# The second attention in sixteen overlapped units, with its half sums added by GpSimd

## What is computed

```python
for Wa, ba in ((W_att0, b_att0), (W_att1, b_att1)):
    kv = bitnet_linear(image_embeds, Wa, ba)          # 361 x 128 for each batch
    k = jnp.concatenate([kv, kv], axis=-1)            # 256 wide, both halves the same
    scores = jnp.einsum('bse,bpe->bsp', fused, k) * inv_sqrt_e
    attn = jax.nn.softmax(scores, axis=-1)
    fused = fused + 0.1 * jnp.einsum('bsp,bpe->bse', attn, k)
```

## Time and profile before

| | us |
|---|---|
| median of 3 runs | 997.46 (996.68 to 1001.53) |
| profiled execution, its own time | 992.82 |
| profiled execution, span from first to last instruction | 991.0 |
| attention, from its first PE instruction to the reduction L1487 | 745.62 to 855.73 |

### The profile page before, as it was taken

The page is one execution under the profiler, slowest core; times in us unless marked ns, Lnnn a source line. Parts: engine busy times, 40 slices in busy tenths (PEclk is TensorE's granted clock), DMA queues, the critical chain, the costliest instruction groups (busy, mean ns, idle before and its releaser), DMA issues.

```text
span 991.0 us, 22346 instructions
## 1 busy us (share of the span) xinstructions
PE 821.7 (83%) x8198; PEld 604.3 (61%) x8198; DVE 725.7 (73%) x1496; ACT 556.1 (56%) x1147; POOL 292.6 (30%) x238
## 2 busy tenths in 40 slices
PE   3777888988898777798899999986647888769995
PEld 2345666666666554587666777772125777549994
DVE  7568787787877898767566776636995666776865
ACT  3446666666665436433555556538975555573542
POOL 3336444353441515040421110007603000053400
PEclk9978999999999777999999999995557888889998
DMA  6423443334453346323275555534200000200002
GB/s 182 106 67 75 97 105 91 100 105 111 121 115 81 82 167 225 110 57 115 74 200 163 163 166 167 142 102 120 71 10 0 2 0 0 85 0 2 3 1 67
DMA packets 76991, 90.47 MB, mean 91 GB/s; under 512 B 22166, under 2 KB 64945, under 8 KB 76842
## 3 DMA queue, kind: packets, MB, share of 16 engines
q1 hardware_dynamic: 69562, 80.95, 29.6%
q0 software_dynamic: 6144, 7.42, 2.8%
q10 hardware_dynamic: 1216, 1.18, 0.4%
HBM read 73.86 MB, written 15.43 MB: 90 GB/s over the span
## 4 chain that ended last, share of the span: by engine, by line
PE 54%; DVE 24%; issue 8%; ACT 7%; DMA 3%; POOL 2%; SPq 1%; ACTq 0%; DVEq 0%; POOLq 0%
PE ps L1151 11%; PE ps L1138 8%; PE ps L337 4%; PE ps L527 4%; PE ps L425 3%; PE ps L1655 3%; PE ps L499 3%; DVE p L515 3%; PE ps L569 3%; DVE m L485 2%; PE ps L2099 2%; PE ps L480 2%; PE ps L1649 2%; PE ps L2110 1%; DVE pmax L1616 1%
## 5 line engine op out<-in xcount | busy, mean ns | idle before, releaser
L485 DVE TENSOR_REDUCE m<-ps 100x2 f32<-100x722 f32 x128 | 115.2, 903 | 52.9 <-PE ps L480 51.3
L506 ACT ACTIVATE p<-ps 128x800 f32<-128x800 f32 x128 | 106.8, 835 | 43.0 <-PE ps L499 40.0
L1200 ACT ACTIVATE hT<-ps,cols 128x500 f32<-128x500 f32 (+1 forms) x96 | 62.5, 651 | 106.4 <-PE ps L1138 98.3
L1151 PE MATMUL ps<-w_h,hT_h 128*125 128x256 f16 (+1 forms) x384 | 105.9, 276 | 7.4 <-DVE x L1247 6.8
L515 DVE SCALAR_TENSOR_TENSOR p<-p 128x600 f32<-128x600 f32 x128 | 107.0, 838 | 0.0
L1207 DVE TENSOR_TENSOR hT_l<-hT,hT_h 128x500 f16<-128x500 f32 (+1 forms) x96 | 62.3, 652 | 60.9 <-ACT hT_h L1201 60.9
L1151 PE MATMUL ps<-w_h,hT_l 128*125 128x256 f16 (+1 forms) x384 | 105.9, 276 | 0.0
L1151 PE MATMUL ps<-w_l,hT_h 128*125 128x256 f16 (+1 forms) x384 | 105.8, 276 | 0.0
L1043 POOL DMA_INDIRECT xe<-tokens,slot_of x32 | 43.1, 1347 | 155.4 <-PE ps L1161 102.1
L1138 PE MATMUL ps<-xe_h,w_h 128*128 128x500 f16 (+1 forms) x192 | 71.7, 374 | 14.3 <-ACT hT_h L1201 6.1
L499 PE MATMUL ps<-qs,ks 128*128 128x100 f16 x768 | 64.7, 215 | 14.3 <-ACT p L506 14.3
(11 more groups left out here) (342 smaller groups left out, 2209.4 us busy)
## 6 DMA issues: line engine op xcount, KB each, us to landing
sw<-in_L_ffn_w_dram SPq DMA_DIRECT2D x16, 512.0 KB, 6.3
sw<-in_L_ffn_w_dram SPq DMA_DIRECT2D x8, 1024.0 KB, 5.9
k_parts<-kp SPq DMA_DIRECT2D x32, 192.0 KB, 2.0
ks<-k_parts SPq DMA_DIRECT2D x32, 192.0 KB
stage<-in_L_xattn_W_f_dram SPq DMA_DIRECT2D x6, 1024.0 KB, 7.4
ctx_f<-in_ctxT_dram SPq DMA_DIRECT2D x16, 270.8 KB, 3.1
stage<-in_ctxT_dram SPq DMA_DIRECT2D x8, 541.5 KB, 8.6
area<-in_ctxT_dram SPq DMA_DIRECT2D x16, 270.8 KB, 6.2
```

Of the source, the lines that this page charges most:

```text
L485: v.tensor_reduce(m32[p][:, 2 * i:2 * i + 2], ps[0:T, at:at + 2, 0:KV], AX.X, ALU.max).then_inc(m_max, 1)
L506: s.activation(p32[:, i % HALF, :, :, :].rearrange("p j n t -> p n j t"), ps[:, t_bank(i):t_bank(i) + 2, 0:(KJ + 1) * T].rearrange("p n (j ...
L1151: i = pe.matmul(bank[4 + j % 3][0:m, 0:C], hTp[p][hh][:, f, j * m:(j + 1) * m], w2p[of][ww][:, f, :], start=(f == 0 and hh == ww), stop=(f ...
L1200: s.activation(hT[:, f % 3, 0:m], bank[2 + f % 2][:, 0:m], ACT.Silu, bias=bias, scale=1.0 / WS)
```

## The change

The attention is written out (no loop) as sixteen units `u` of two batches and one round. `unit_of(u)` gives the pair of batches and the round: units 0 and 1 are pairs 0 and 1 with `r` = 0, units 2 and 3 the same pairs with `r` = 1, and so on. On PE the list of a unit is: scores of `u`; product of values and probabilities of `u` - 1 (both batches into one of banks 6 and 7); values, then keys, of `u` + 1; transposes of `u`. ACT's list is: exponentials of `u`, keys of `u` + 1, copies of `u`. DVE's is: scores of `u`, normalise the first batch, update `fused` for `u` - 1 (one instruction for both batches), normalise the second batch, values of `u` + 1. The tiles of a unit are two of the four (`at_slot`). `f12` is made by POOL, one 128 x 200 addition for a unit, in two buffers. The four additions of `x_b2_gpsimd` stand behind `f12` of units 3, 5, 7 and 9. The roundings of batches 8, 10, 12 and 14 on ACT and 5 to 15 on DVE stand inside the attention, behind given units (`ROUND_ACT`, `ROUND_DVE`). The maximum over `fused` is split: the last group of four batches is taken in two halves, and that of the image averages is taken ahead of the attention. The diff, where the bodies that the listing above shows are cut:

```diff
@@ -1451,9 +1451,13 @@
         neg_s = [over_vis(T, KV) for _ in range(Q)]
         prob = [over_vis(T, KP) for _ in range(Q)]
         probT = [over_vis(KT, KJ, T) for _ in range(Q)]
-        f12 = [over_vis(128, T) for _ in range(Q)]
+        f12 = [over_vis(128, 2 * T) for _ in range(2)]
         small = over_vis(T, 3, Q)
         txt_q = over_vis(128, CC * NTOK // 2).bitcast(F16).rearrange("p (c n) -> p c n", c=CC)
+
+        UNITS = B
+        ROUND_ACT = {2: 8, 4: 10, 6: 12, 8: 14}
+        ROUND_DVE = {0: 5, 1: 7, 3: 9, 4: 11, 6: 13, 8: 15}
 
         ULP = 2.0 ** -24
         CTX, VIS, IMG_, TEXT, CAT, HID = range(6)
@@ -1617,100 +1621,163 @@
                             ).then_inc(c_pm, 1)
 
 
+        def unit_of(u):
+
+            return 2 * (u // 4) + u % 2, u % 4 // 2
+
+        def pair_tokens(pair):
+            return slice(2 * pair * T, 2 * (pair + 1) * T)
+
+        def at_slot(u, q):
+            return 2 * (u % 2) + q
+
         def att_tensor(pe):
-            def body(t, *_):
...
+            def keys_values(u):
+                if u == UNITS:
+                    return
+                pair, r = unit_of(u)
+                if u % 4 == 0:
+                    pe.wait_ge(c_p1, B // 2 + B + u // 2 + 2)
+                    pe.wait_ge(c_q, B // 2 + u // 2 + 2)
+                for q in range(2):
+                    b = 2 * pair + q
+                    wait(pe, n_ve, 2 * (u - 1) + q + 1)
+                    for j in range(KJ):
                         for k in range(CC):
-                            i = pe.matmul(bank[q][:, 0:KV], w_q[ATT + r][:, k, :],
...
+                            i = pe.matmul(bank[2 + q][0:KT, j * 128:(j + 1) * 128],
+                                          img_q[:, k, b * KV + j * KT:b * KV + (j + 1) * KT], w_q[ATT + r][:, k, :],
+                                          start=(j == 0 and k == 0), stop=(k == 1), skip_group_check=True)
+                    i.then_inc(n_v, 1)
+                for q in range(2):
+                    b = 2 * pair + q
+                    wait(pe, n_sc, 2 * (u - 1) + q + 1)
+                    for k in range(CC):
+                        i = pe.matmul(bank[q][:, 0:KV], w_q[ATT + r][:, k, :], img_q[:, k, b * KV:(b + 1) * KV],
+                                      start=(k == 0), stop=(k == 1))
+                    i.then_inc(n_k, 1)
+
+            def values_out(u):
+                if u < 0:
+                    return
+                wait(pe, n_u, u - 1)
+                for q in range(2):
+                    pe.wait_ge(n_ve, 2 * u + q + 1)
+                    pe.wait_ge(n_pte, 2 * u + q + 1)
+                    for j in range(KJ):
+                        i = pe.matmul(bank[6 + u % 2][:, q * T:(q + 1) * T], kvt[at_slot(u, q)][:, j, :],
+                                      probT[at_slot(u, q)][:, j, :], start=(q == 0 and j == 0), stop=(j == KJ - 1),
+                                      skip_group_check=True)
+                i.then_inc(n_o, 1)
+
+            keys_values(0)
+            for u in range(UNITS):
+                pe.wait_ge(n_f, u + 1)
+                for q in range(2):
+                    pe.wait_ge(n_ke, 2 * u + q + 1)
+                    pe.matmul(bank[q][0:T, 0:KV], f12[u % 2][:, q * T:(q + 1) * T], kvT[at_slot(u, q)],
+                              start=True, stop=True).then_inc(n_s, 1)
+                values_out(u - 1)
+                keys_values(u + 1)
+                for q in range(2):
+                    pe.wait_ge(n_p, 2 * u + q + 1)
+                    for j in range(KJ):
+                        i = pe.transpose(bank[4 + q][0:KT, j * T:(j + 1) * T],
+                                         prob[at_slot(u, q)][:, j * KT:(j + 1) * KT], ident[0:T, 0:T])
+                    i.then_inc(n_t, 1)
+            values_out(UNITS - 1)
 
         def att_scalar(s):
-            def body(t, *_):
...
+            def keys(u):
+                if u == UNITS:
+                    return
+                r = unit_of(u)[1]
+                for q in range(2):
+                    s.wait_ge(n_k, 2 * u + q + 1)
+                    s.activation(kvT[at_slot(u, q)], bank[q][:, 0:KV], ACT.Identity,
+                                 scale=oscale[:, ATT + r:ATT + r + 1], bias=col(f"L1_xattn_b_att{r}")).then_inc(n_ke, 1)
+
+            keys(0)
+            for u in range(UNITS):
+                for q in range(2):
+                    at = at_slot(u, q)
+                    s.wait_ge(n_sc, 2 * u + q + 1)
+                    s.activation(prob[at][:, 0:KV], neg_s[at], ACT.Exp, scale=-1.0, bias=small[:, 0, at:at + 1],
+                                 accum_out=small[:, 1, at:at + 1]).then_inc(n_e, 1)
+                keys(u + 1)
+                for q in range(2):
+                    s.wait_ge(n_t, 2 * u + q + 1)
+                    s.copy(probT[at_slot(u, q)], bank[4 + q][0:KT, 0:KJ * T].rearrange("p (j t) -> p j t", j=KJ)
+                           ).then_inc(n_pte, 1)
+                if u in ROUND_ACT:
+                    round_scalar(s, IMG_, img_f, img_q, 128, ROUND_ACT[u])
+
+        def att_gpsimd(g):
+
+            g.wait_ge(h_ev, 8)
+            for u in range(UNITS):
+                pair, r = unit_of(u)
+                tok = pair_tokens(pair)
+                wait(g, n_s, 2 * (u - 1))
+                if r == 1:
+                    g.wait_ge(n_u, u - 1)
+                g.tensor_tensor(f12[u % 2], fused[:, 0, tok], fused[:, 1, tok], ALU.add).then_inc(n_f, 1)
+                if u in (3, 5, 7, 9):
+                    x_b2_gpsimd(g, (u - 3) // 2)
 
         def att_vector(v):
-            def body(t, *_):
...
+            def values(u):
+                if u == UNITS:
+                    return
+                r = unit_of(u)[1]
+                for q in range(2):
+                    v.wait_ge(n_v, 2 * u + q + 1)
+                    v.scalar_tensor_tensor(kvt[at_slot(u, q)],
+                                           bank[2 + q][0:KT, 0:KJ * 128].rearrange("p (j c) -> p j c", j=KJ),
+                                           oscale[0:KT, ATT + r:ATT + r + 1],
+                                           att_b[r][:, None, :].broadcast_to((KT, KJ, 128)),
+                                           ALU.mult, ALU.add).then_inc(n_ve, 1)
+
+            def normalise(u, q):
+                at = at_slot(u, q)
+                v.wait_ge(n_e, 2 * u + q + 1)
+                v.reciprocal(small[:, 2, at:at + 1], small[:, 1, at:at + 1]).then_inc(n_r, 1)
+                v.wait_ge(n_r, 2 * u + q + 1)
+                v.tensor_scalar(prob[at][:, 0:KV], prob[at][:, 0:KV], small[:, 2, at:at + 1], None,
+                                ALU.mult).then_inc(n_p, 1)
+
+            def update(u):
+                if u < 0:
+                    return
+                tok = pair_tokens(unit_of(u)[0])
+                v.wait_ge(n_o, u + 1)
+                v.scalar_tensor_tensor(fused[:, :, tok], bank[6 + u % 2][:, None, 0:2 * T].broadcast_to((128, CC, 2 * T)),
+                                       0.1, fused[:, :, tok], ALU.mult, ALU.add).then_inc(n_u, 1)
+
+            def fused_max(column, lo, hi):
+                return v.tensor_reduce(pmax[:, column:column + 1], fused[:, :, lo * T:hi * T], AX.XY, ALU.max,
+                                       apply_absolute_value=True)
+
+            values(0)
+            for u in range(UNITS):
+                for q in range(2):
+                    at = at_slot(u, q)
+                    v.wait_ge(n_s, 2 * u + q + 1)
+                    v.tensor_scalar(neg_s[at], bank[q][0:T, 0:KV], -float(C) ** -0.5, None, ALU.mult, ALU.min,
+                                    accum_out=small[:, 0, at:at + 1]).then_inc(n_sc, 1)
+                normalise(u, 0)
+                update(u - 1)
+                normalise(u, 1)
+                values(u + 1)
+                if u in ROUND_DVE:
+                    round_vector(v, IMG_, img_f, img_q, 128, ROUND_DVE[u])
+                if u % 4 == 1 and u > 4:
+                    v.wait_ge(n_u, u - 1)
+                    fused_max(u // 4 - 1, u // 4 * 4 - 4, u // 4 * 4)
+            v.wait_ge(n_u, UNITS - 1)
+            fused_max(3, B - 4, B - 2)
+            update(UNITS - 1)
+            v.wait_ge(n_u, UNITS)
+            vs.inc(fused_max(5, B - 2, B))
 
         def layer2_tensor(pe):
             lin_tensor(pe, 0, w_q[D2V], ctx_q)
@@ -1783,13 +1850,13 @@
                 v.scalar_tensor_tensor(x[:, b:b + 2, :], y_bank(b)[0:T, :].rearrange("p (b c) -> p b c", b=2),
                                        oscale[0:T, F2:F2 + 1], x[:, b:b + 2, :], ALU.mult, ALU.add).then_inc(y_ev, 2)
 
-        def x_b2_gpsimd(g):
...
+        def x_b2_gpsimd(g, n):
+
+            if n == 0:
+                g.wait_ge(c_b_in, 48)
+                g.wait_ge(ln_xn, 3 * B)
+            part = x[:, LB * n:LB * (n + 1), :]
+            g.tensor_tensor(part, part, f2_b[:, None, :].broadcast_to((T, LB, C)), ALU.add).then_inc(x_bias, 1)
 
         def last_stats(v, g):
 
```

(14 more changed lines are left out.)

89 lines of the change are left out of this document (removed).

## The result

The kernel became faster: median 970.2 us (965.5 to 974.5, four runs) against 997.1 on the same chip, ratio 0.9727 with an interval of 0.9689 to 0.9765. By the ratio that is 27.2 us, between 23.4 and 31.0; the two medians lie 26.8 apart. The profiled execution took 974.49, its span 972.7.

What follows compares the result with a forecast made beforehand. PE, the busiest engine, was held to lose one wait on DVE per block plus the clock, the larger part. Ideal gain 28.3 - 0.8 - 3.0 - 2.1 = 22.4 us; 997.46 - 22.4 = 975.1, with 971 to 980 likeliest (0.60), 968 to 987 at 0.85.

Steps and rivals of the forecast that it cites:

- near ideal: Rival for the total time: at most 2 us of the deductions arise, giving 969 to 971 us; chance 0.08.
- The unit: PE's products for one attention unit at the upper clock sum to 4.92 us, 78.7 us for sixteen.
- Everything else keeps up: In each unit DVE (3.8 us) and ACT (3.5 us) stay below PE's 4.92; roundings moved in cost nothing.
- The clock: TensorE's clock falls after some PE waits in the attention, making a slow block about 3.4 us longer.
- slower: Rival: in PE's dense stream the clock falls every other unit; ten falls give 11.6 us slower, 1009; chance 0.05.
- The rival of two to four falls: Rival: the clock still falls two to four times, losing 7 to 14 us: 982 to 989 us; chance 0.10.
- f12 on POOL: POOL's f12 delays the second normalisation on DVE by 0.5 us in eight units, mostly slack: 0.8 us in all.
- The handoffs: A result PE really waits for costs 0.14 us more; one in each unit, 2.1 us.
- The maxima: Maxima on DVE inside the attention, about 1 us three times, fit beside PE's work and cost nothing.
- The additions: POOL's bias additions behind f12 of units 5 and 9 hold DVE's second multiply, 1.5 us each: 3.0 us.
- The ports cost their bounds: Rival: POOL's additions and DVE's multiplies block each other, leaving 12.3 us of gain: 985 us; chance 0.12 for 980 to 987.
- It doesn't overlap as it says: Rival: the loop of update, POOL and scores is longer than a unit, so no change; chance 0.05.

Runs made afterwards that it cites:

- the filled kernel: Kernel before, with twenty small unused products on PE behind each block's scores: stage 98.02 us, median 976.2, ratio 0.986.
- additions of almost nothing: POOL's four bias additions cut to 2 of 256 channels: changed kernel, stage 80.32 us, ratio 0.971; same cut in the kernel before, stage 106.44, ratio 0.998.
- The rearranged kernel: Changed kernel with f12 on DVE, DVE's roundings ahead of the attention, bias additions behind units 3, 6, 10, 11: stage 78.01 us, ratio 0.967.
- the additions moved: Changed kernel with POOL's four bias additions behind f12 of units 3, 6, 10 and 11, f12 staying on POOL: stage 80.33 us, ratio 0.970.
- the kernel with the units alone: Changed kernel with f12 on DVE, roundings and bias additions ahead of the attention as in the kernel before: stage 81.22 us, ratio 0.971.

## Why the prediction was right, by its own steps

The kernel became faster, and the median of 970.2 lies in the range of 968 to 987 that was given 0.85. It lies 0.8 us under the range of the likeliest case (971 to 980), where the "near ideal" rival had 969 to 971; but that rival wanted at most 2 us of deductions, and 9.1 arose. The stage came out 1.7 us under the 87.7 that the sum gave (110.11 - 22.4), from errors of both signs: a unit put too long and deductions put too small. That they nearly cancel is luck. The gain of the medians is 26.8 us, of which the stage shows 24.1; the other 2.7 lie within what the untouched stages vary by.

| step | predicted | measured |
|---|---|---|
| unit without waits | 4.92 | 4.51 to 4.57 |
| start to unit 1's scores | 6.2 | 6.16 |
| unit 15's scores to the reduction | 6.7 | 7.16 |
| fourteen steps between | 68.9 + 5.9 of deductions | 63.6 + 9.1 |
| stage | 87.7 | 85.97 |

- **The unit** is the mis-sized term: 14 x 0.38 = 5.3 us too long. I took the transposes as 2 x 2.07/4 from the earlier trace rows. But there each followed DVE's next tile. In the chain after, six take 0.62. In the kernel before, the four multiplies of that block end 0.51 us apart (797.96 to 799.50), and each three transposes start 0.15 behind one. The record of a group that is fed by another engine was read as a cost of its own; the rate at which the tiles came would have shown it.
- **Everything else keeps up**: right where neither POOL nor a maximum comes between. From 810 to 820 PE is busy 10.00 of 10 us. The update at 569 ns against 0.57 was right too. Over the whole stage PE is busy 90%, at 0.98, where I had named over 95% at 1.00 as the sign of being right.
- **The clock**: its fall in three blocks came of PE's wait, as the earlier trace rows suggested, and the filled kernel shows it. A slow block was 3.1 us longer than a fast one by my own figures (14.5 against 11.4), not the 3.4 that I used; the "slower" rival then needs 7.2 falls instead of 6.6. With the wait gone the stage has clock 1.00 but for the fall at the end of unit 7 and in unit 8. The rival of two to four falls came in at one, in two profiles of three.
- **f12 on POOL**, 0.8 us: somewhat too small. It took 0.60 to 0.61 in nearly all units where I had 0.56, and it held just the eight multiplies that I laid out, by 0.44 us each where I had 0.5 (additions of almost nothing). The rearranged kernel, which has neither this nor late additions, is 2.3 us below the one with additions of almost nothing (80.32 to 78.01); with the additions moved, taking f12 off POOL gave 1.0. The first difference holds DVE's roundings too, so 1.0 to 2.3 it is, net of what f12 costs on DVE.
- **The handoffs**, 2.1 us: in a unit without a late tile PE's pieces join without a gap (chain after), so nothing.
- **The maxima**, put at nothing: 0.7 to 1.0 us. Units 6, 10 and 14 are 0.24 each longer than the 4.54 of the others in the kernel with the units alone, and 0.38, 0.38 and 0.24 in the rearranged one. Each stands right behind a maximum; that the maximum is the cause is read from this order, no run leaves it out. With additions of almost nothing the fourteen steps are 67.0, 3.4 above 63.6: that is f12, the roundings and the maxima together, near the 2.9 that I had for f12 and the handoffs, and near it by chance.
- **The additions**, 3.0 us: 5.65 in this profile, 4.0 in the second (84.33 to 80.33), 7.0 in the third. I gave 1.5 each to those behind f12 of units 5 and 9, and that was right: the first costs unit 3 1.45, and with the roundings taken out of the attention the second costs unit 7 the same 1.45. I gave nothing to the one behind f12 of unit 7, on a layout where DVE only reads PSUM beside it. That layout left out the rounding that stands in unit 6: it was held 1.6 us, all of unit 7 came late on DVE, and the next addition met its first multiply instead of its second. This made unit 7 another 1.2 to 1.5 us longer, and the clock fell behind it in two profiles of three. Each edit was costed by itself, and each was free by itself: the rounding with almost no additions beside it (unit 7 4.5), the addition with the roundings elsewhere (unit 6 5.20, as with almost no additions).
- **"The ports cost their bounds"** came in half: its sign was there (L1684 waited 6.1 us for L1745), its 16.0 us of deductions were not. The deductions were 9.1, between the forecast's 5.9 and these.
- **"It doesn't overlap as it says"** and **"slower"** found no support: scores waited on POOL in the opening (0.93 us) and hardly elsewhere, and PE's dense stretches kept the clock at 1.00.

The row of L391 decided between 0.56 us and the Trainium skill's advice (GPSIMD Engine Reference, section Engine selection) to leave two-input additions to VectorE. The same addition took 0.60 us on POOL and 0.36 on DVE: not a factor of two, but the advice was right here, for the multiplies beside it went from 408 to 519 ns (612 with the bias additions too). What held them agrees with the Trainium skill's SBUF — State Buffer, section Who interferes with whom, by which some VectorE operations and a GpSimd operation exclude each other for a whole instruction, whichever is first: the multiply of 790.70 ended 0.2 us behind the addition.

Still open is why the same wait of 1.6 us in unit 7 was followed by a fall of the clock in two profiles and not in the third; no run varied it alone. In the kernel before too, single waits of 1.25 us were followed by a fall in some blocks (772.49, 809.57, 823.88) and not in others (786.80, 838.11), and those of 1.51 in none of two (798.11, 849.43), so the length of the wait by itself doesn't tell.

## What to carry to other kernels

When PE's chain leaves it once in each block, put another unit's products into that gap: it takes away the wait and with it the clock's fall, and here the units were 28.9 of 110 us; filling the gap with products of no use was 12.1 already. Before moving small work to GpSimd, lay all its pieces and DVE's SBUF-to-SBUF multiplies, roundings and additions on one time axis: where they meet costs more than what they take, and a held instruction that nobody waits for can make the next ones meet another addition at a worse place. Take a duration from a stretch where its engine isn't being fed tile by tile.

## What the runs showed of the hardware

- Twenty products of no use in PE's wait (1.28 us a block) made the kernel before 12.1 us shorter in the stage, and only in the blocks where the clock had fallen: idle time that looked free was the dearest in the stage.
- Beside POOL's additions of 2.4 us, three SBUF-to-SBUF forms of DVE stretched to the end of them (rounding 0.59 to 2.21, multiply 0.41 to 1.58 and 1.83, addition 0.25 to 1.88), while those with PSUM as a source kept their 0.57 and 0.60. Not all SBUF-to-SBUF forms are held: in the rearranged kernel and in the one with the additions moved a maximum over 128 x 800 lay wholly beside such an addition and took its 0.97, and the reciprocals beside one (769.49 in unit 3) kept 0.15.
- Fp32 transposes of 100 x 121 take 0.10 us each on PE in a row, and 0.17 by the record when DVE feeds them.
- POOL's idle time between the cross-partition maximum and its next addition (7.22 us in the earlier trace rows) is there for a tiny addition just as well: 7.25.
